# Two edits to the order of work in a transformer kernel's delta-rule phase: a normalisation placed 16 scan instructions earlier on VectorE, and gate products threaded between output products on GpSimd

## The chip, the cores and the metric

One core of one Trainium2 chip runs the whole program. The metric is device time in microseconds (us) of one execution. The kernel before takes 1597.2 us, the median of three runs (1592.9 to 1600.5).

Engines are called PE (TensorE, matmuls and transposes), DVE (VectorE), ACT (ScalarE), POOL (GpSimd) and SP (SyncE, which issues the DMAs). Each executes its own list of instructions in the order in which it was written; they meet only through semaphores.

## The reference

The input is `x` of shape (8, 512, 128). Two layers, each an attention and a feed-forward part, each followed by `layernorm(x + part(x))`:

```
x = ln(x + attention16(x))            # softmax attention, 16 heads of 8
x = ln(x + soft_moe(x))               # 8 experts x 64 slots, gelu
x = ln(x + delta_block(x))            # below
x = ln(x + ternary_mlp(x))            # silu(x W1)*(x W2) -> gelu(. H1) -> gelu(. H2) -> W3
```

`delta_block` holds the only part that is serial in time. For every batch and head a state `S` of 8 x 8 is carried over the 512 time steps:

```
S = S + beta * outer(k, v - S^T k);   o = S^T q
h = x + o @ Wo;   y = rmsnorm(h)
h = h + (silu(y @ Wg) * (y @ Wu)) @ Wd
```

The change touches only the last two lines of the model, which the kernel does together as its second phase.

## The kernel before, in words

Phase one (the first 950 us) does attention and the mixture of experts, batch by batch. The change leaves it as it is.

Phase two handles the 512 time steps in eight blocks of 64. The blocks are worked in a software pipeline of ten steps. While step `t` runs, these blocks are in work:

- **block t: the scan** (DVE, `scan`, lines 1746 to 1782). The 128 batch-head pairs lie on the partitions. The block is cut into 16 chunks of 4 time steps. 12 instructions (L1752 to L1765) prepare all chunks, then every chunk takes 6 dependent ones (L1770, L1772, L1773, L1775, L1777, L1781): 108 in all. Below, n is the count of scan instructions already issued in a step. The state lies in PSUM and ACT copies it away in four quarters (`keep_history`, L1428 and L1429). DVE may overwrite a quarter's state only when it has been copied (semaphore `hist_kept`).
- **block t-1: output and first MLP.** POOL multiplies the kept states with q (`out_products`, L734 and L736; `half` 1 is the second half of the block), DVE sums them (`sum_out`, L1795), SP sends the result through DRAM to transpose it (L577, L581), PE projects it (use `wo`, L1093), DVE adds the residual and makes the factor of the rmsnorm (`residual_h`, L1806 on), POOL applies it (L755), PE transposes (use `hT`), and PE, ACT and POOL do the gated MLP: PE `gates_gu` (L1102), ACT copies (L1378), POOL `gate_gu` (L750), PE `mlp_out` (L1108). PE then does one quarter of another block's layer (`layer_n(last, 3)`, L1116) and transposes the result, use `fo` (`turn_f`, L1085). DVE adds it in `norm_x3` (L1820) and makes the statistics of the layernorm; ACT applies them; PE transposes `x3`.
- **block t-2, called `last`: second MLP.** PE `gates_ab` (L1102), POOL `gate_ab` (L744, one for each quarter `c` of the hidden width), PE `layer_m` for k = 0 to 3, where quarter k waits for `gate_ab` of c = k, then `layer_n`, `last_out`, `turn_y`; DVE `norm_x4` (L1828).

PE's list for a step is: `gates_ab`, `layer_m` 0 to 3, `layer_n` 0 and 1, `project_o` (use `wo`), `layer_n` 2, `turn_h`, `gates_gu`, `mlp_out`, `layer_n` 3, `turn_f`, `last_out`, `turn_y`, `turn_x3`.

On DVE the pieces stand between the scan's instructions at places that are numbers. In its `step`:

```
upto(AT_PAIRS)                 # scan up to n = 12
... sum_out(mlp, 1, r), sum_scores, norms_qk with scan between
upto(AT_H);  residual_h(...)   # n = 31
upto(AT_F);  norm_x3(...)      # n = 83
norm_x4(...)                   # 12 scan instructions threaded through it
upto(AT_S);  sum_out(scanned, 0, r) x4, one scan instruction after each
further(DVE_SCAN)              # the rest
```

`norm_x3` waits for `fo` on PE, and everything behind it on DVE, the scan too, stands still while it waits. `norm_x4` is called with scan instructions between its own dependent ones, `norm_x3` without.

POOL's list for a step is: four `gate_ab` of `last`, four `out_products` of half 1 of block t-1 (the first waits for the fourth quarter of `hist_kept`, so for the end of that block's scan), then `score_products` (L721), `squares2` (L698), `normalise` (L707 to L712), `normalise_h` (L755), four `gate_gu`, and four `out_products` of half 0.

Of the kernel before, what the change touches and what calls it, by code (L numbers as in the profile page):

```python
# [32 lines left out]
HC = HID // P  # L33
QW = 3 * D + NH
CH = 4
# [104 lines left out]
def build(nc, A, out, taps=None):  # L140
    ctx = ExitStack()
    with ctx:
# [477 lines left out]
        def _(g):  # L620
# [73 lines left out]
            def squares2(t, h):  # L694
                g.wait_ge(l_loaded[h], CREDIT + (t - h) * 32 + 64)

                g.wait_ge(norms_done, CREDIT + t * DVE_NORMS)
                g.tensor_tensor(l_sq, mix[:, h, 0:2 * HD, :], mix[:, h, 0:2 * HD, :], ALU.mult).then_inc(l_squared, 1)  # L698

            def normalise(t, h):  # L700


                g.wait_ge(norms_done, CREDIT + (t + 1) * DVE_NORMS)
                r_q, r_k = l_r[:, 0:TS], l_r[:, TS:2 * TS]
                by_time = lambda j: mix[:, h, j * HD:(j + 1) * HD, :].rearrange("p d t -> p t d")
                along = lambda r: r.unsqueeze(2).broadcast_to([P, TS, HD])
                g.tensor_tensor(k_c, by_time(1), along(r_k), ALU.mult).then_inc(l_kb, 1)  # L707
                g.tensor_tensor(wu[h][:, :, 0:HD], by_time(1), along(r_beta), ALU.mult).then_inc(l_kb, 1)
                g.tensor_tensor(wu[h][:, :, HD:2 * HD], by_time(2), along(beta[:, h, :]), ALU.mult).then_inc(l_kb, 1)
                g.tensor_tensor(k_d[:, h, :, :], mix[:, h, HD:2 * HD, :], r_k.unsqueeze(1).broadcast_to([P, HD, TS]),  # L710
                                ALU.mult).then_inc(l_kb, 1)
                g.tensor_tensor(q_c[:, h, :, :], by_time(0), along(r_q), ALU.mult).then_inc(l_kb, 1)  # L712

            def score_products(t, h):

                g.wait_ge(l_kb, CREDIT + (t + 1) * 5)
                g.wait_ge(qkd_done, CREDIT + t)
                qc = q_c[:, h, :, :].rearrange("p (c j) d -> p c j d", j=CH)
                kc = k_c.rearrange("p (c j) d -> p c j d", j=CH)
                for r, at in PAIRS:  # L720
                    last = g.tensor_tensor(qk_m[:, :, at:at + r + 1, :], kc[:, :, 0:r + 1, :],  # L721
                                           qc[:, :, r, :].unsqueeze(2).broadcast_to([P, NC, r + 1, HD]), ALU.mult)
                last.then_inc(qk_made, 1)

            def out_products(t, h, half, r):

                cs = slice(half * HALF, (half + 1) * HALF)
                if r == 0:
                    g.wait_ge(hist_kept, CREDIT + t * 4 + 2 * half + 2)
                    g.wait_ge(om_summed, CREDIT + t * 8)  # L730
                    g.wait_ge(qkd_done, CREDIT + t + 1)
                qc = q_c[:, h, :, :].rearrange("p (c j) d -> p c j d", j=CH)
                _, at = PAIRS[r]
                g.tensor_tensor(o_m[half][r][:, :, :, 0:HD], state[h][:, cs, :, :],  # L734
                                qc[:, cs, r, :].unsqueeze(2).broadcast_to([P, HALF, HD, HD]), ALU.mult)
                g.tensor_tensor(o_m[half][r][:, :, :, HD:HD + r + 1], u_c[h][:, cs, :, 0:r + 1],  # L736
                                qkd[:, h, cs, at:at + r + 1].unsqueeze(2).broadcast_to([P, HALF, HD, r + 1]), ALU.mult) \
                    .then_inc(om_made, 1)

            def gate_ab(t, c):  # L740
                if c == 0:
                    g.wait_ge(a2_ready, CREDIT + t * len(A2.order))
                g.wait_ge(a2_act, CREDIT + A2.emptied(f"b{c}", t))
                g.tensor_tensor(hid_a[:, c, :], up[:, c % 2, :], gate[:, c % 2, :], ALU.mult).then_inc(gated2, 1)  # L744

            def gate_gu(t, c):
                if c == 0:
                    g.wait_ge(a1_ready, CREDIT + t * len(A1.order))
                g.wait_ge(a1_act, CREDIT + A1.emptied(f"u{c}", t))
                g.tensor_tensor(hid_g[:, c, :], up[:, c % 2, :], gate[:, c % 2, :], ALU.mult).then_inc(gated1, 1)  # L750

            def normalise_h(t, h):

                g.wait_ge(h_done, CREDIT + (t + 1) * DVE_H)
                g.tensor_tensor(hn, h1, st_h[:, 5, :].unsqueeze(2).broadcast_to([P, 4, D]), ALU.mult).then_inc(hn_done, 1)  # L755
                g.tensor_tensor(x2t[h], x2t[h], h1, ALU.add).then_inc(x2_added, 1)

            def step(scan, after, mlp, last, h):
                if last is not None:
                    for c in range(HC):  # L760
                        gate_ab(last, c)
                if mlp is not None:
                    for r in range(CH):
                        out_products(mlp, 1 - h, 1, r)
                if scan is not None:
                    score_products(scan, h)
                if after is not None:
                    squares2(after, 1 - h)
                    normalise(after, 1 - h)
                if mlp is not None:  # L770
                    normalise_h(mlp, 1 - h)
                    for c in range(HC):
                        gate_gu(mlp, c)
                if scan is not None:
                    for r in range(CH):
                        out_products(scan, h, 0, r)

            squares2(0, 0)
            normalise(0, 0)
            step(0, 1, None, None, 0)  # L780
            step(1, 2, 0, None, 1)
            with g.Fori(0, 2) as i:
                step(2 * i + 2, 2 * i + 3, 2 * i + 1, 2 * i, 0)
                step(2 * i + 3, 2 * i + 4, 2 * i + 2, 2 * i + 1, 1)
# [1099 lines left out]

QK_TURNED = (1, 3)

AT_PAIRS, AT_H, AT_F, AT_S = 12, 31, 83, 90

W_FIRST = 4 + 4 + 1 + 2 + 1 + 1
W_REST = 2 + 2 + 2 + 4 + 2 + 2 + 2 + 2 + 4  # L1890
# [29 lines left out]
```

## Time and profile before

| | us |
|---|---|
| median of three runs | 1597.2 |
| the profiled execution, device time | 1600.5 |
| its span in the trace | 1598.8 |
| phase two in the trace, first scan instruction to the end | 950.7 to 1598.8 |

The profiled execution is one of the three runs, the slowest. Its steps 1 to 7 of phase two begin at 1004.9, 1072.3, 1143.1, 1217.8, 1289.8, 1361.9 and 1433.2 us; the last scan ends at 1495.8. All times inside the text are microseconds from the start of the span. Where a row is a timeline row, its first number is when the instruction began and the second how long it took; what stands in brackets is how long the engine was idle before it, and what ended that.

### The profile page before, as it was taken

Reading aid. Unit: us, or ns where it says so; the run is one execution under the profiler, and the core shown is the slowest. Engines: PE = TensorE matmul, PEld = TensorE weight load, DVE = VectorE, ACT = ScalarE, POOL = GpSimd, SP = SyncE. Lnnn points to the kernel's source line nnn. Section 1 sums busy time; section 2 is a strip of 40 time slices with the busy share of each in tenths; the row PEclk is TensorE's granted clock in tenths of the full one; section 3 lists DMA queues with packets and bytes.
Section 4 is the critical chain, followed back from the end, with each engine's and each line's share of the span. In section 5 each row is a group of like instructions: output and inputs, shape, how many; then the busy total and the mean of one; then the engine's idle time right before and its main releaser. Section 6 shows DMA issues by size and latency. Waiting matters only on the chain.

```text
span 1598.8 us, 18446 instructions
## 1 busy us (share of the span) xinstructions
PE 1192.1 (75%) x5332; PEld 589.3 (37%) x5332; DVE 990.2 (62%) x2506; ACT 618.3 (39%) x1167; POOL 464.7 (29%) x460
## 2 busy tenths in 40 slices
PE   2288888798888989889796510178977788799987
PEld 1133345363453535445353300033433343333433
DVE  1162835637576374863636239988988899998520
ACT  1115081652817437174363200032534435254452
POOL 0103031210302113030110033555654565555230
PEclk9557597896978969789698755588989889899999
DMA  4302011021201112021000041010101100000000
GB/s 140 105 1 93 8 41 60 1 93 35 85 15 58 62 34 92 7 67 52 28 1 28 28 102 21 13 28 14 28 24 38 35 20 7 20 7 20 20 0 14
DMA packets 81365, 61.72 MB, mean 39 GB/s; under 512 B 40720, under 2 KB 60816, under 8 KB 81296
## 3 DMA queue, kind: packets, MB, share of 16 engines
q1 hardware_dynamic: 81296, 60.92, 13.0%
q8 instruction: 29, 0.48, 0.1%
q14 instruction: 40, 0.33, 0.1%
HBM read 34.69 MB, written 25.95 MB: 38 GB/s over the span
## 4 chain that ended last, share of the span: by engine, by line
PE 44%; DVE 23%; issue 14%; ACT 8%; POOL 8%; DMA 2%; SPq 1%; DVEq 0%; ACTq 0%; POOLq 0%
PE ps L1102 5%; DVE arena L1584 5%; PE ps L813 5%; PE ps L1116 4%; PE ps L875 4%; PE ps L845 3%; ACT arena L1252 3%; PE ps L1108 3%; ACT arena L1214 3%; PE ps L864 2%; PE ps L924 2%; PE ps L848 2%; PE ps L951 2%; PE ps L904 2%; PE ps L942 2%
## 5 line engine op out<-in xcount | busy, mean ns | idle before, releaser
L1214 ACT ACTIVATE arena<-ps 128x512 f32<-128x512 f32 (+2 forms) x200 | 109.9, 573 | 384.2 <-PE ps L813 305.9
L1116 PE MATMUL ps<-arena,f_h 128*128 128x512 f32 x512 | 230.0, 606 | 0.0
L1584 DVE TENSOR_REDUCE arena<-ps 128x2 f32<-128x1024 f32 (+3 forms) x176 | 194.8, 1123 | 36.5 <-PE ps L848 33.3
L668 POOL TENSOR_SCALAR_AFFINE_SELECT arena<-arena 128x512 f32<-128x512 f32 x128 | 84.3, 659 | 386.6 <-ACT arena L1252 386.2
L1252 ACT ACTIVATE arena<-ps 128x1024 f32<-128x1024 f32 (+3 forms) x256 | 170.1, 718 | 38.8 <-PE ps L864 37.3
L845 PE MATMUL ps<-kr,qr 32*128 32x512 f32 (+3 forms) x512 | 123.6, 534 | 48.5 <-DVE arena L1584 24.1
L813 PE MATMUL ps<-ident,arena 128*128 128x128 f32 (+1 forms) x640 | 112.0, 323 | 62.2 <-DVE arena L1525 27.6
L1116 PEld LDWEIGHTS ps<-arena,f_h 128*128 128x128 f32 x512 | 99.6, 196 | 123.3 <-issue 123.3
L1378 ACT ACTIVATE arena<-ps,f_s 128x512 f32<-128x512 f32 x128 | 85.4, 688 | 89.7 <-PE ps L1116 72.3
L1629 DVE RECIPROCAL arena<-ps 128x16 f32<-128x16 f32 x32 | 8.2, 256 | 172.3 <-PE ps L813 172.2
L813 PEld LDWEIGHTS ps<-ident,arena 128*128 128x128 f32 (+1 forms) x640 | 82.2, 159 | 88.3 <-issue 32.5
L875 PE MATMUL ps<-arena 128*32 128x512 f32 (+3 forms) x1024 | 100.0, 476 | 16.5 <-ACT arena L1214 16.5
L1378 ACT ACTIVATE arena<-ps 128x512 f32<-128x512 f32 x96 | 57.0, 597 | 129.7 <-PE ps L1085 56.1
L1093 PE MATMUL ps<-w_o,arena 128*128 128x128 f32 x64 | 13.6, 380 | 120.6 <-DMA arena<-o_d 120.6
L845 PEld LDWEIGHTS ps<-kr,qr 32*128 32x128 f32 x512 | 57.0, 248 | 103.3 <-DVE arena L1584 71.6
L864 PE MATMUL ps<-qr,kr 32*128 32x256 f32 (+3 forms) x512 | 74.2, 435 | 27.9 <-ACT arena L1252 21.5
L734 POOL TENSOR_TENSOR arena<-arena 128x512 f32<-128x512 f32 x64 | 86.2, 1347 | 29.9 <-ACT e_w L1429 29.9
L1616 DVE TENSOR_REDUCE arena<-ps 128x1 f32<-128x512 f32 x64 | 44.1, 689 | 79.9 <-PE ps L904 75.2
L864 PEld LDWEIGHTS ps<-qr,kr 32*128 32x128 f32 x512 | 34.7, 194 | 120.4 <-ACT arena L1252 91.2
L1102 PE MATMUL ps<-arena,f_w 128*128 128x512 f32 x128 | 71.6, 723 | 5.7 <-ACT arena L1378 5.7
L848 PE MATMUL ps<-mask_qk,ident_b 128*128 128x128 bf16 (+2 forms) x352 | 75.7, 313 | 0.0
L744 POOL TENSOR_TENSOR arena<-arena 128x512 f32<-128x512 f32 x32 | 41.1, 1283 | 106.1 <-ACT arena L1378 97.0
(168 smaller groups left out, 2083.6 us busy)
## 6 DMA issues: line engine op xcount, KB each, us to landing
qr<-q_rep SPq DMA_DIRECT2D x8, 1024.0 KB, 5.7
kr<-k_rep SPq DMA_DIRECT2D x8, 1024.0 KB, 7.9
q_rep<-hilo SPq DMA_DIRECT2D x24, 256.0 KB, 3.0
k_rep<-hilo SPq DMA_DIRECT2D x24, 256.0 KB, 3.8
proj_d<-arena SPq DMA_DIRECT2D x8, 768.0 KB, 3.6
arena<-proj_d SPq DMA_DIRECT2D x24, 256.0 KB, 4.1
arena<-in_L_ffn_h_w SPq DMA_DIRECT2D x2, 1024.0 KB, 8.6
arena<-in_L_attn_x SPq DMA_DIRECT2D x8, 256.0 KB, 2.8
```

What stands on the lines that cost most here:

```text
L734: g.tensor_tensor(o_m[half][r][:, :, :, 0:HD], state[h][:, cs, :, :], qc[:, cs, r, :].unsqueeze(2).broadcast_to([P, HALF, HD, HD]), ALU.mult)
L813: last = pe.transpose(bank[0:src.shape[1], k * P:(k + 1) * P], src, ident[:, :])
L845: pe.matmul(bank[:, j, :], qr[rows, gg, it * P:(it + 1) * P], kr[rows, gg, 0:w], start=(j == 0), stop=False)
L848: last = pe.matmul(bank[:, :, it * P:w], ident_b[:, :], mask_qk[:, :].unsqueeze(1).broadcast_to([P, len(gs), P]), start=False, stop=True)
L864: last = pe.matmul(ps[:, 2 * (k % 2) + n, 0:S - jt * P], kr[rows, gg, jt * P:(jt + 1) * P], qr[rows, gg, jt * P:S], start=True, stop=True)
L875: last = pe.matmul(bank[32 * h4:32 * h4 + 32, jt * P:S], v_aug[:, jt, 4 * gg + h4, :], prob[:, gg % 2, h4, p_off[jt]:p_off[jt] + S - jt * ...
L1102: return pe.matmul(ps[:, ring2.bank(use), :], w, src, start=True, stop=True)
L1116: last = pe.matmul(ps[:, ring2.bank(f"{n}{c}"), :], w[:, k, c * P:(c + 1) * P], src[:, k, :], start=(k == 0), stop=(k == HC - 1))
L1214: return act.activation(dst, src(ps[:, bank, :]), func, **kw)
L1252: act.activation(prob[:, gg % 2, 2 * pr:2 * pr + 2, p_off[jt]:p_off[jt] + w], ps[:, bank:bank + 2, 0:w], ACT.Exp).then_inc(p_taken, 1)
L1378: return act.activation(dst, src(ps[:, ring2.bank(use), :]), func, **kw)
L1584: v.tensor_reduce(heads[:, 2 * pr:2 * pr + 2, gs[0]:gs[-1] + 1], ps[:, 2 * (k % 2):2 * (k % 2) + 2, 0:len(gs) * w].rearrange("p q (n w) -> ...
```

## The change

On POOL, the four `gate_ab` of `last` no longer all stand ahead of the `out_products` of half 1. Two stand ahead, the third comes behind the first product pair and the fourth behind the second. On DVE the place of `norm_x3` goes from n = 83 to n = 67.

```diff
@@ gpsimd step @@
-                if last is not None:
-                    for c in range(HC):
+                for c in range(2):
+                    if last is not None:
                         gate_ab(last, c)
-                if mlp is not None:
-                    for r in range(CH):
-                        out_products(mlp, 1 - h, 1, r)
+                for c in range(4):
+                    if mlp is not None:
+                        out_products(mlp, 1 - h, 1, c)
+                    if last is not None and c < 2:
+                        gate_ab(last, c + 2)
@@ constants @@
-AT_PAIRS, AT_H, AT_F, AT_S = 12, 31, 83, 90
+AT_PAIRS, AT_H, AT_F, AT_S = 12, 31, 67, 90
```

POOL, second step of the loop, before (L744 is `gate_ab`, L734 and L736 are one `out_products`, the REGISTER_ALU rows make the number of a semaphore wait):

```order
L743 REGISTER_ALU
L744 TENSOR_TENSOR arena<-arena 128x512
L729 REGISTER_ALU
L734 TENSOR_TENSOR arena<-arena 128x64x8
L736 TENSOR_TENSOR arena<-e_w,arena 128x64
L734 TENSOR_TENSOR arena<-arena 128x64x8
L736 TENSOR_TENSOR arena<-e_w,arena 128x64x2
```

The same place now:

```order
L729 REGISTER_ALU
L734 TENSOR_TENSOR arena<-arena 128x64x8
L736 TENSOR_TENSOR arena<-e_w,arena 128x64
L743 REGISTER_ALU
L744 TENSOR_TENSOR arena<-arena 128x512
L734 TENSOR_TENSOR arena<-arena 128x64x8
L736 TENSOR_TENSOR arena<-e_w,arena 128x64x2
```

The gate product now stands behind the wait (L729) that belongs to the first output product.

DVE, around `norm_x3` in an early step, before (L1773 to L1777 are the third to fifth instruction of a chunk of the scan, L1820 is the first of `norm_x3`):

```order
L1773 TENSOR_TENSOR ps<-arena,ps 128x32
L124 REGISTER_ALU
L1775 TENSOR_TENSOR arena<-ps,arena 128x256
L124 REGISTER_ALU
L1777 TENSOR_REDUCE arena<-arena 128x64
L1729 REGISTER_ALU
L1820 TENSOR_TENSOR arena<-ps,arena 128x512
```

Now, with every line number two higher because the file has two lines more (L1783 is the last instruction of a chunk, L1772 the first of the next, L1822 is `norm_x3`):

```order
L1783 TENSOR_TENSOR ps<-ps,arena 128x64
L124 REGISTER_ALU
L1772 TENSOR_TENSOR arena<-arena,ps 128x256
L1731 REGISTER_ALU
L1822 TENSOR_TENSOR arena<-ps,arena 128x512
L1823 REGISTER_ALU
L1502 BN_STATS arena<-arena 128x6 x4
```

`norm_x3` and, behind it, `norm_x4` moved ahead of 16 scan instructions. Nothing was added or taken away on any engine.

## Rows read from the trace of the kernel before

**Rows 1.** The page: the chain that ended last, shares of the span by engine

```profile
PE 44%; DVE 23%; issue 14%; ACT 8%; POOL 8%; DMA 2%; SPq 1%; DVEq 0%; ACTq 0%; POOLq 0%
```

**Rows 2.** Busy time in step 3: PE, PEld, DVE, ACT, POOL, clock, DMA, GB/s

```profile
1143.00:1218.00 75.00, 63.00 (x144) 27.52 (x143) 66.19 (x181) 30.82 (x59) 42.66 (x39) 0.89 0.10 26
```

**Rows 3.** DVE's waits from 1072 to 1496: total, times, longest

```profile
DVE slot_T L1808 <- ACT arena L1407: 8.1, 6, 1.3
...
DVE arena L1800 <- POOL arena L721: 0.8, 1, 0.8
DVE arena L1820 <- PE ps L1085: 0.6, 1, 0.6
DVE arena L1738 <- POOL arena L698: 0.4, 1, 0.4
```

**Rows 4.** DVE's timeline, step 3: end of residual_h, n=67, n=83, norm_x3

```profile
1174.99 0.16 DVE L1491 SCALAR_TENSOR_TENSOR slot_T<-slot_T 128x4 f32<-128x4 f32 x1
...
1189.07 0.42 DVE L1770 TENSOR_TENSOR arena<-arena,ps 128x256 f32<-128x256 f32 x1
...
1195.38 0.42 DVE L1777 TENSOR_REDUCE arena<-arena 128x64 f32<-128x256 f32 x1
1195.93 0.69 DVE L1820 TENSOR_TENSOR arena<-ps,arena 128x512 f32<-128x512 f32 x1
```

**Rows 5.** PE's timeline, step 3: layer_n 3 and the transposes of fo

```profile
1191.86 3.60 PE L1116 MATMUL ps<-arena,f_h 128*128 128x512 f32 x8
1195.29 0.60 PE L1085 MATMUL ps<-ident,arena 128*128 128x128 f32 x4
```

**Rows 6.** The same pair, PE's fo and DVE's norm_x3, in steps 1, 5, 7

```profile
1050.52 0.66 PE L1085 MATMUL ps<-ident,arena 128*128 128x128 f32 x4 [0.69 <-ACT arena L1378]
1054.76 0.68 DVE L1820 TENSOR_TENSOR arena<-ps,arena 128x512 f32<-128x512 f32 x1
...
1341.53 0.60 PE L1085 MATMUL ps<-ident,arena 128*128 128x128 f32 x4
1342.39 0.68 DVE L1820 TENSOR_TENSOR arena<-ps,arena 128x512 f32<-128x512 f32 x1
...
1476.00 0.60 PE L1085 MATMUL ps<-ident,arena 128*128 128x128 f32 x4
1477.75 0.68 DVE L1820 TENSOR_TENSOR arena<-ps,arena 128x512 f32<-128x512 f32 x1
```

**Rows 7.** POOL's and ACT's timelines around the end of step 3's scan

```profile
1213.07 1.27 POOL L744 TENSOR_TENSOR arena<-arena 128x512 f32<-128x512 f32 x1 [0.44 <-ACT arena L1378]
1214.98 0.27 ACT L1429 ACTIVATE e_w<-ps 128x128 f32<-128x128 f32 x1
1215.50 1.26 POOL L734 TENSOR_TENSOR arena<-arena 128x512 f32<-128x512 f32 x1 [1.16 <-ACT e_w L1429]
...
1223.09 4.13 POOL L721 TENSOR_TENSOR arena<-arena 128x128 f32<-128x128 f32 x4
```

**Rows 8.** PE's timeline, step 4: layers m and n, then project_o

```profile
1212.11 20.76 PE L1116 MATMUL ps<-arena,f_h 128*128 128x512 f32 x48
1239.96 2.07 PE L1093 MATMUL ps<-w_o,arena 128*128 128x128 f32 x8 [7.10 <-DMA arena<-o_d]
```

**Rows 9.** PE in a window: length, busy, granted clock, DMA share, GB/s

```profile
1252.00:1259.00 7.00, 6.24 (x10) 0.52 0.00 0
```

**Rows 10.** PE's and DVE's timelines, step 8: layers, project_o, last sum

```profile
1495.02 20.76 PE L1116 MATMUL ps<-arena,f_h 128*128 128x512 f32 x48
1515.62 1.05 PE L1093 MATMUL ps<-w_o,arena 128*128 128x128 f32 x8
...
1504.15 0.95 DVE L1795 TENSOR_REDUCE arena<-arena 128x64 f32<-128x768 f32 x1 [0.98 <-POOL arena L736]
```

**Rows 11.** DVE's timeline: first three scan instructions of steps 4, 7

```profile
1217.82 2.79 DVE L1752 TENSOR_TENSOR arena<-arena 128x128 f32<-128x128 f32 x3 [3.15 <-issue]
...
1433.18 1.09 DVE L1752 TENSOR_TENSOR arena<-arena 128x128 f32<-128x128 f32 x3
```

## The prediction

> **What bounds the kernel now.** I read the page first, then the busy windows of phase two step by step, then DVE's waits, then the timelines of DVE, PE, POOL and ACT around the two places of the change.
>
> The page's chain gives PE the largest share [rows 1], but that is an average over two phases, and most of PE's part is phase one, which is not touched. In a step of phase two DVE is busy 66.2 of 75 us, PE 63.0 and POOL 42.7 [rows 2]; the rest of DVE's time is mostly the short gap between one scan instruction and the next that needs it. So the question is whether DVE waits for anyone. Between 1072 and 1496 it hardly does [rows 3]: 8.1 us for ACT inside `residual_h` (1.3 each time), and 0.6 us once for PE in front of `norm_x3`. Phase two up to the end of the last scan is bound by DVE's list, and whatever makes DVE stand still there is added to the time, unless a wait further down gives it back.
>
> **The DVE edit: the new wait.** What `norm_x3` waits for is `fo`. In step 3 `residual_h` ends at 1174.99 + 0.16 = 1175.15, and `fo` is ready at 1195.29 + 0.60 = 1195.89 [rows 4, 5]: 20.7 us later, by way of POOL, PE, ACT, POOL and again PE. DVE fills this with scan. It issues n = 83 at 1195.38, ends it at 1195.80, and begins `norm_x3` at 1195.93 [rows 4], with 0.04 us between the end of `fo` and that start. The place is filled to the brim: DVE arrives when `fo` does.
>
> At n = 67 it arrives earlier: the 67th scan instruction ends at 1189.07 + 0.42 = 1189.49 [rows 4], 14.3 us behind the end of `residual_h`, and the 83rd at 1195.80. The 16 between take 6.31 us. Nothing in the edit makes `fo` come sooner: its chain begins at n = 31, whose place is the same. It needs the scan only up to n = 60 (ACT copies the second quarter of the state ahead of its copy for `fo`), and 60 is below 67, so the chain can go on while DVE stands. The new wait is therefore 6.31 us less whatever room there was between the end of `fo` and the start of L1820:
>
> - step 1: `fo` at 1051.18, L1820 at 1054.76 [rows 6], room 3.6: wait 2.7. There is no `last` block in work yet, so PE has no `layer_n` 3 (3.6 us [rows 5]) in front of `fo`.
> - step 2: L1820 already waits 0.6 [rows 3]; it will wait 6.9: 6.3 more.
> - step 3: room 0.04: 6.3.
> - step 5: `fo` at 1342.13, L1820 at 1342.39 [rows 6], room 0.26: 6.05. Steps 4 and 6 are like it; I take 6.1 and 6.2.
> - step 7: `fo` at 1476.60, L1820 at 1477.75 [rows 6], room 1.15: 5.2, treated with the tail.
>
> Steps 1 to 6 give 2.7 + 6.3 + 6.3 + 6.1 + 6.05 + 6.2 = 33.6 us. The amount of work behind the place is the same, since `norm_x4` still threads 12 scan instructions and the four sums one each, so nothing is gained by threading. What is late next is each following step as a whole: DVE's scan ends 6 us later relative to its `residual_h`.
>
> Can it be given back? Only by a wait of DVE that shrinks. All waits of rows 3 are tied to things that DVE itself started shortly before (the 1.3 us for ACT's squares) and shift with it. I count nothing.
>
> **The POOL edit inside the loop.** Before, the fourth gate product begins at 1213.07 and ends at 1214.34; the state's last quarter has been copied at 1215.25, and the first output product starts at 1215.50 [rows 7], 0.8 us behind the scan's end (1214.7). So the gates were through before the wait that now stands in front of two of them. With the scan's end 6.3 us later relative to the gates, the first product starts at about 1221.8 on that clock, the third gate is through 1.6 + 1.2 us later at 1224.6, the fourth 1.8 + 1.2 us later at 1227.6. PE has `layer_m` 0 and 1 done by 1212.11 + 16 x 0.43 = 1219.0 (0.43 us for each of the 48 instructions [rows 8]) and now stands 5.6 us in front of `layer_m` 2. The 32 instructions left then end at 1224.6 + 13.8 = 1238.4. `project_o` waits for its DMA, which follows DVE's sums, and so starts 6.3 us later than before, at 1246.3; it had 7.10 us of idle PE ahead [rows 8] and still has 7.9. The price on the path is 0; the cover is that gap, and if it were used up, each us beyond would delay `residual_h`'s input.
>
> POOL is behind by the two gates, 2.5 us, for the output products 2 to 4 and `score_products`, which began at 1223.09 [rows 7]. DVE has waited for that line and for L698 once, 0.8 and 0.4 us [rows 3], in step 2, where POOL's first output product was 2 us late. Bounds: 0 and 1.2 us in each of six steps, 0 to 7 us; the waits of the steps where POOL was on time are 0, but the margin is under 1 us in the loop, so I take 2 us.
>
> The gates also move beside DVE's 12 preparing instructions, which read SBUF as POOL does. These are unsteady: the first three take 2.79 us in step 4 and 1.09 in step 7 [rows 11]. POOL was already busy without a gap from 1215.50 on, so it is other POOL work that is pushed out behind them. Gain and loss are both possible, 1.7 us a step either way by rows 11, and I take 0. The Trainium skill ("SBUF — State Buffer", section "Who interferes with whom") says that a DVE instruction with two SBUF inputs and a GpSimd instruction exclude each other for the whole instruction. By that rule each of the two gates could hold up one DVE instruction for up to its 1.27 us, 2.5 us a step or 15 us in six; rows 11 agree that such collisions happen, and for the sum they only matter if they are more than before.
>
> **The tail.** Behind the last scan PE is the bound: in step 8 its 48 instructions end and `project_o` starts at 1515.62 [rows 10] although DVE's last sum was done at 1505.1, and the way through DRAM took 5.1 us from such an end (1234.8 to 1239.96 in step 4), so the data were there at about 1510.2. Here the wait of step 7 is partly covered, but the gates are not. With DVE 5.2 us late the scan ends at 1501.0. `layer_m` could start 1.1 us earlier than the 1495.02 of rows 10, and its quarter 2 at 1493.9 + 6.9 = 1500.8; instead gate 2 is through 0.7 + 1.5 + 1.25 us behind the scan's end (products and gates as in rows 7, less the collisions with the scan, which is over), 1504.4. 32 instructions of 0.43 end at 1518.2. The data side: the last product is through at 1501.0 + 0.7 + 6.9 + 2.5 = 1511.1, its sum at 1512.1, its data at 1517.2. `project_o` starts at 1518.2 and not 1515.6: +2.6 us, and all that follows is serial.
>
> **Sum.** 33.6 + 2 + 2.6 = 38 us on the profiled execution's 1600.5, so 1638.7. That execution is 3.3 us above the median of the runs shown, so the median becomes 1597.2 + 38 = 1635. A change of less than 0.5% (8 us) can't be told from none here.
>
> **Rivals.**
> - **PE's clock stays up (faster than my sum, still slower than before).** After idle stretches the granted clock is low: 0.52 in 1252 to 1259 [rows 9], 1.2 GHz, right after 4.6 us of idle PE, just in the chain to `fo`. In step 7 and 8, where it was mostly at 2.4 GHz there, the chain took 19.2 and 18.9 us and not 20.3 to 21.2. If the shifted pauses spared the chain, the waits of steps 2 to 6 would be 1.2 us shorter each: 1635 - 6 = 1629. Against it: the idle time between `project_o` and the transposes of `hn` does not change. The new pause of 5.6 us in front of `layer_m` 2 may lower the clock there; that lengthens work with 7.9 us to spare, and in the tail adds up to 3 us. The Trainium skill ("TensorE: Matmul & The Clock Gate", section "HAM oscillation — how this bites in real kernels") says that a pause between bursts makes the next burst start at the low clock every time; rows 9 agree with it. By that rule the new pause costs in the tail, which stands inside my range.
> - **POOL becomes a second wait.** The backlog of 2.5 us reaches DVE at L1800 or L1738 in every step (7 us and not 2), and collisions cost 1.3 us a step more (8 us): 1635 + 5 + 8 = 1648. For it: step 2, where POOL was late, and rows 11. Against it: from step 3 on POOL was ready each time.
> - **Not slower.** One mechanism: `fo` comes by the time that DVE reaches n = 67, because its chain takes at most 14.3 us. Then the wait is 0 and x3 is in hand 6.3 us earlier, the tail could start 1.1 us sooner, and the time is about 1596. It decides at 14.3 us. Against it: the shortest chain in the trace is 16.7 us (step 1, 1051.18 less 1034.5), without `layer_n` 3, and no instruction of the chain is taken out or moved.
>
> **How the numbers follow.** My forecast (1628 to 1643 by itself, each term within its bounds) 0.68; clock 0.13; POOL 0.14; not slower 0.05, of which faster 0.02 and within 0.5% 0.03. Slower by over 0.5%: 0.95. The range reaches from under the clock case to above the POOL case, 1620 to 1651, and leaves out some 1 in 8.
>
> **What would show it.** In the profile after, DVE's waits should have a row of `norm_x3` (L1822) waiting for PE's L1087, about 7 times and 57 us, of which 19 were there in step 8. The steps 2 to 6 should be 78 us long and not 72. PE should pause about 5 us between the second and the third quarter of `layer_m`, released by POOL's L744. In step 8 `project_o` should start about 17 to 18 us behind the last scan's end. If L1822 waits much less, the chain to `fo` became shorter and I am wrong on the main term; if DVE waits for POOL at L1802 or L1740 the second rival is at work; if `project_o` is late inside the loop, the spare 7.9 us was wrong.

## The result, and the profile after

The changed kernel takes 1638.6 us (median of four runs, 1637.8 to 1641.1) against 1598.4 us before (four runs): ratio 1.026, 95% interval 1.023 to 1.029. It is slower by 40 us; 38 us had been predicted.

The page of the kernel after, for all engines and for the chain that ended last:

```profile
PE 1196.0 (73%) x5332; PEld 588.4 (36%) x5332; DVE 994.8 (61%) x2506; ACT 618.5 (38%) x1167; POOL 463.5 (28%) x460
...
PE 42%; DVE 23%; issue 15%; POOL 8%; ACT 8%; DMA 2%; SPq 1%; DVEq 0%; ACTq 0%; POOLq 0%
```

The chain's shares are those of [rows 1] within two points: nothing in such a page tells where 40 us went. All lines of DVE and most others are numbered two higher than before. The waits of DVE from the first step to behind the last scan do tell it (line, who was waited for, total, times, longest):

```profile
DVE arena L1822 <- PE ps L1087: 36.9, 7, 6.8
DVE slot_T L1810 <- ACT arena L1409: 9.4, 7, 1.3
...
DVE arena L1830 <- PE ps L1087: 3.0, 6, 0.5
DVE arena L1802 <- POOL arena L721: 2.0, 1, 2.0
```

`norm_x3` (L1822) waits in each of the seven steps, 36.9 us in all; before it was 0.6 us in one step [rows 3]. DVE's timeline in step 3 shows one of these waits, between the 67th scan instruction and `norm_x3`:

```profile
1201.83 0.42 DVE L1772 TENSOR_TENSOR arena<-arena,ps 128x256 f32<-128x256 f32 x1
1208.80 0.69 DVE L1822 TENSOR_TENSOR arena<-ps,arena 128x512 f32<-128x512 f32 x1 [6.55 <-PE ps L1087]
```

and PE's timeline what it waits for, the last quarter of layer n and then the transposes of `fo`:

```profile
1204.73 3.60 PE L1118 MATMUL ps<-arena,f_h 128*128 128x512 f32 x8
1208.16 0.60 PE L1087 MATMUL ps<-ident,arena 128*128 128x128 f32 x4
```

`fo` is ready at 1208.76, 20.8 us behind the end of `residual_h` (1187.9), where it was 20.7 us in [rows 4, 5]. The chain to `fo` is as long as it was; DVE comes to it earlier and stands.

The other edit shows in POOL's timeline at the end of the same scan (1233.9). The two later gates (L744) now stand behind a product pair each:

```profile
1234.75 1.26 POOL L734 TENSOR_TENSOR arena<-arena 128x512 f32<-128x512 f32 x1 [11.05 <-ACT e_w L1431]
1235.97 0.33 POOL L736 TENSOR_TENSOR arena<-e_w,arena 128x64 f32<-128x64 f32 x1
1236.26 1.26 POOL L744 TENSOR_TENSOR arena<-arena 128x512 f32<-128x512 f32 x1
...
1239.41 1.58 POOL L744 TENSOR_TENSOR arena<-arena 128x512 f32<-128x512 f32 x1
```

and in PE's, which pauses for the first of them and still has time to spare in front of `project_o` (L1095); before, 48 instructions ran without a pause [rows 8]:

```profile
1224.90 7.03 PE L1118 MATMUL ps<-arena,f_h 128*128 128x512 f32 x16
1237.58 7.75 PE L1118 MATMUL ps<-arena,f_h 128*128 128x512 f32 x14 [5.65 <-POOL arena L744]
...
1258.68 2.07 PE L1095 MATMUL ps<-w_o,arena 128*128 128x128 f32 x8 [5.63 <-DMA arena<-o_d]
```

Phase one, which is the same code in all these kernels, ends anywhere between 945 and 954 us from one profile to the next. So profiles are compared below by phase two alone, from the first scan instruction to the end of the span: 648.1 us before (950.7 to 1598.8), 686.4 after (953.0 to 1639.4), 38.3 us more.

### The profile page after: what moved, and what is told of

The parts are those of the page before. It is cut to its first block, busy times and chain, and to the rows that moved or that the text cites. A ratio compares the mean times of both kernels' runs of the same rounds, so it can differ in the third digit from the quotient of the medians.

```text
span 1639.4 us, 18446 instructions
## 1 busy us (share of the span) xinstructions
PE 1196.0 (73%) x5332; PEld 588.4 (36%) x5332; DVE 994.8 (61%) x2506; ACT 618.5 (38%) x1167; POOL 463.5 (28%) x460
## 4 chain that ended last, share of the span: by engine, by line
PE 42%; DVE 23%; issue 15%; POOL 8%; ACT 8%; DMA 2%; SPq 1%; DVEq 0%; ACTq 0%; POOLq 0%
PE ps L1104 5%; DVE arena L1586 5%; PE ps L815 4%; PE ps L1118 4%; PE ps L877 4%; PE ps L847 3%; PE ps L1110 3%; ACT arena L1216 3%; ACT arena L1254 3%; PE ps L866 2%; PE ps L926 2%; PE ps L906 2%; PE ps L850 2%; PE ps L953 2%; PE ps L944 2%
## 5 line engine op out<-in xcount | busy, mean ns | idle before, releaser
L1118 PE MATMUL ps<-arena,f_h 128*128 128x512 f32 x512 | 242.3, 630 | 40.6 <-POOL arena L744 40.6
L1118 PEld LDWEIGHTS ps<-arena,f_h 128*128 128x128 f32 x512 | 102.9, 204 | 172.8 <-issue 125.3
L734 POOL TENSOR_TENSOR arena<-arena 128x512 f32<-128x512 f32 x64 | 85.9, 1342 | 98.5 <-ACT e_w L1431 98.5
L1095 PE MATMUL ps<-w_o,arena 128*128 128x128 f32 x64 | 11.0, 325 | 112.5 <-DMA arena<-o_d 112.5
L1087 PE MATMUL ps<-ident,arena 128*128 128x128 f32 x128 | 23.8, 316 | 67.3 <-POOL arena L755 44.0
L1104 PE MATMUL ps<-arena,f_w 128*128 128x512 f32 x128 | 67.8, 690 | 5.7 <-ACT arena L1380 5.7
```

Source lines behind the costliest of these rows:

```text
L1104: return pe.matmul(ps[:, ring2.bank(use), :], w, src, start=True, stop=True)
L1118: last = pe.matmul(ps[:, ring2.bank(f"{n}{c}"), :], w[:, k, c * P:(c + 1) * P], src[:, k, :], start=(k == 0), stop=(k == HC - 1))
```

## The experiments

The question for the first four is: is the loss DVE's wait, what does POOL's order do, and what sets the length of the wait.

**1. Only the DVE edit.** From the kernel before:

```diff
-AT_PAIRS, AT_H, AT_F, AT_S = 12, 31, 83, 90
+AT_PAIRS, AT_H, AT_F, AT_S = 12, 31, 67, 90
```

> The kernel before with norm_x3 at n = 67 and POOL's order as it was. Theory (DVE waits at norm_x3 for a fo that comes no sooner): waits of 2.7, 6.3, 6.3, 6.1, 6.05, 6.2 us in steps 1 to 6 and 5.2 in step 7, the last hidden in the tail where PE is the bound, which gains 1 us; 33.6 - 1 = 33 us more than before, about 1631 us. Rival (a good part of the 40 us comes from the POOL order, because PE then stands 36 us in all for gate products): under 1620 us.

Measured: 1637.1 us, ratio 1.0246 (1.0227 to 1.0265); phase two 684.9 us, 36.8 more than before. The rival is out: this edit alone is nearly the whole loss. It is 6 us more than expected. DVE's waits in this run:

```profile
DVE arena L1820 <- PE ps L1085: 37.5, 7, 6.0
```

33.4 of the 37.5 us lie in steps 1 to 6, against 33.6 expected plus the 0.6 that was there, so the main term was right. What was missed is in the 12 preparing scan instructions: in step 2 they took 8.8 us before and 11.8 here (see experiment 8). In step 1 the chain to `fo` took 18.2 us and not 16.7, at a mean granted clock of PE of 0.75 and not 0.82, which cost 1.5. The two make 4.4 of the 6 us. About 2 us more fell in step 5, where two instructions of `norm_x4` on 128 x 4 elements took 1.25 and 1.14 us beside gate products on POOL, instead of 0.15 each.

**2. Only the POOL edit.** From the changed kernel, with the place of `norm_x3` set back:

```diff
-AT_PAIRS, AT_H, AT_F, AT_S = 12, 31, 67, 90
+AT_PAIRS, AT_H, AT_F, AT_S = 12, 31, 83, 90
```

> The kernel before with only POOL's gate products threaded between output products, norm_x3 at n = 83. Theory: the gates still come before layer_m needs them or cost only spare PE time, the sums in the tail come 2.5 us later with 5 us to spare: 1598 us, no change within 2 us. Rival (POOL order carries a good part of the loss by itself): 1605 to 1620 us, with PE pauses in front of layer_m of over 3 us a step.

Measured: 1596.1 us, ratio 0.9994 (0.9981 to 1.0006): no change, as the theory had it. In this run PE has no wait for a gate product in any row of the waits from 1072 to 1500. By itself the reordering costs nothing that the times show, since the gates are there before PE wants them. POOL's delay does reach DVE: it waits twice 2.0 us for the score products (L721), where it waited 0.8 us once before.

**3. norm_x3 at n = 75**, half way, POOL as before:

```diff
-AT_PAIRS, AT_H, AT_F, AT_S = 12, 31, 83, 90
+AT_PAIRS, AT_H, AT_F, AT_S = 12, 31, 75, 90
```

> The kernel before with norm_x3 at n = 75, half way. Theory: the place is 3.15 us of scan earlier, less the room: 0 in step 1, 3.15, 3.1, 2.9, 2.9, 3.0 in steps 2 to 6, tail -1: 14 us more than before, about 1612 us. Rival (the cost is that of DVE's order as such, not of time standing in front of fo): not in proportion, near 1598 or near the 1631 of n = 67.

Measured: 1619.4 us, ratio 1.0124 (1.0103 to 1.0146). DVE's wait:

```profile
DVE arena L1820 <- PE ps L1085: 18.6, 7, 3.5
```

0.6, 18.6, 37.5 us at n = 83, 75, 67: the wait grows in proportion to the scan taken away in front of it, and the time with it (0, 20, 39 us by the ratios). The expected 14 us were too few by the first two things of experiment 1: step 1 waits 1.5 us, and the 12 preparing instructions of step 2 take 11.8.

**4. Both edits, and the last quarter of layer n behind fo on PE:**

```diff
                 if mlp is not None:
                     mlp_out(mlp, turn)
-                if last is not None:
-                    layer_n(last, turn, 3)
                 if mlp is not None:
                     turn_f(mlp, turn)
                 if last is not None:
+                    layer_n(last, turn, 3)
                     last_out(last, turn)
```

> The changed kernel (both edits) with PE's last quarter of layer n put behind the transposes of fo instead of ahead. Theory (the wait is as long as the chain from residual_h to fo, and these 3.6 us of PE stand in it, of which 2.5 are not hidden by ACT's copy): fo 2.5 us sooner in steps 2 to 8, waits of about 3.7 us and not 6.2, 12.5 us less in the loop and 2.5 to 5 less in the tail: about 1622 us. Rival (the chain is held by something else, POOL or the end of the scan): 1636 to 1640 us.

Measured: 1645.0 us, ratio 1.0291 (1.0273 to 1.0309), so 6 us slower than the change and not 17 us faster. The expected effect on `fo` is there, in step 3 it comes 18.3 us behind `residual_h` and not 20.8. DVE's waits (its lines are one higher than before in this kernel):

```profile
DVE arena L1821 <- PE ps L1087: 25.2, 7, 4.4
DVE arena L1829 <- PE ps L1087: 12.5, 6, 2.2
```

The first wait fell by 11.7 us, and the second, of `norm_x4` for `y`, rose by 9.5 (3.0 after the change). `y` needs the moved quarter as well; in step 3 it now comes 0.9 us later, since PE pauses 0.69 us for ACT's copy in front of `fo`. And `norm_x3`, started sooner, now runs beside POOL's output products: from its start to the end of the scan it is 28.6 us in steps 2 to 5, and 25.1 in the changed kernel. DVE's timeline in step 3:

```profile
1209.15 0.39 DVE L1505 TENSOR_TENSOR slot_T<-arena 128x4 f32<-128x4 f32 x1
1209.47 1.31 DVE L1506 TENSOR_TENSOR slot_T<-arena 128x4 f32<-128x4 f32 x1
1210.71 0.72 DVE L1507 TENSOR_TENSOR slot_T<-arena 128x4 f32<-128x4 f32 x1
```

Three instructions that take 0.16 us each in the kernel before take 2.4 us together. My theory of a single wait fell: DVE has two things to wait for there, and shortening the way to the first hands most of the wait on. The rival fell too, since the time rose above its 1640 us.

**5. The same on the kernel before** (n = 83), to see the second part alone:

> The kernel before with PE's last quarter of layer n behind the transposes of fo, norm_x3 at n = 83. In the run with both edits this made fo 2.4 us sooner and the time 6 us longer. Theory A (fo is only the first of two things that DVE waits for here; y, for norm_x4, comes 0.8 us later since PE now pauses for ACT's copy of fT): DVE waits 0.8 us a step more for y, about 1603 us. Theory B (fo alone counts): no change in the loop and 2.5 us gained in the tail, 1595 us.

Measured: 1603.7 us, ratio 1.0038 (1.0023 to 1.0052), the time of theory A. `fo` came up to 4.7 us before DVE wanted it. DVE's wait for `y` in the kernel before and in this one:

```profile
DVE arena L1828 <- PE ps L1085: 2.0, 5, 0.5
...
DVE arena L1827 <- PE ps L1085: 4.6, 5, 1.8
```

So fewer than the 0.8 us a step of theory A: 1.3 us more in step 2, 0.8 in step 3, 0.3 or less from step 4 on, 2.6 us in all. Phase two is 3.9 us longer (652.0 against 648.1). Up to the start of step 7 it is 1.6 us; the rest came behind it, where the 12 preparing instructions took 12.4 us and not 9.4. Theory B is out, but the time agrees with theory A partly by luck.

**6. Use the time instead: scan instructions threaded through norm_x3**, at n = 83. The call is given the same threading that `norm_x4` has:

```diff
-                    norm_x3(mlp, 1 - h, order(ln3_done, DVE_LN, mlp, False))
+                    norm_x3(mlp, 1 - h, order(ln3_done, DVE_LN, mlp, True))
```

> The kernel before with 12 scan instructions threaded through norm_x3, at n = 83. Theory (DVE's list bounds the loop and norm_x3's small dependent instructions waste their gaps): norm_x3 to norm_x4 takes 4.8 us and 12 scan instructions 4.7 us; threaded together 6.4 us as norm_x4 does; 3.1 us less in each of 7 steps, 2 us more in the tail and up to 1 us a step for POOL coming later: 1580 to 1586 us. Rival (the circle of PE, ACT and POOL from residual_h back to residual_h takes over): 1593 us or more, with DVE waiting for project_o.

Measured: 1613.8 us, ratio 1.0114 (1.0086 to 1.0141). The theory fell, and so did the rival's account of it. DVE waits 0.3 us in all for `fo` and not at all for `project_o` in the loop. It waits here:

```profile
DVE ps L1781 <- ACT e_w L1429: 37.0, 7, 6.0
```

L1781 is the last instruction of the scan. It overwrites the third quarter of the state, which ACT must have copied. ACT's timeline at the end of step 3's scan (1216.2) shows where that copy (L1428, L1429) stood:

```profile
1203.48 1.65 ACT L1412 ACTIVATE arena<-arena,slot_T 128x128 f32<-128x128 f32 x4 [2.41 <-DVE slot_T L1815]
...
1214.82 0.69 ACT L1378 ACTIVATE arena<-ps,f_s 128x512 f32<-128x512 f32 x1 [0.17 <-PE ps L1102]
1215.41 0.38 ACT L1428 ACTIVATE arena<-ps 128x256 f32<-128x256 f32 x1
1215.67 0.28 ACT L1429 ACTIVATE e_w<-ps 128x128 f32<-128x128 f32 x1
```

It is behind the six ACT copies for `gate_ab` (L1378), which follow from `norm_x3` itself. In the kernel before that copy ended 2.7 us ahead of L1781 (1211.7 against 1214.4 in step 3). Threaded, DVE can reach L1781 5.2 us sooner behind the start of `norm_x3` (13.5 us and not 18.7 to the end of the scan; experiment 9 shows it without the wait), and the copy ends 3.1 us later behind that start, 2.1 of them since ACT gets the statistics later. 5.2 + 3.1 - 2.7 is the 5.6 us that DVE waits in step 3. The wait belongs to neither edit of the change.

**7. residual_h threaded as well**, `norm_x3` at n = 91:

```diff
-                    residual_h(mlp, 1 - h, order(h_done, DVE_H, mlp, False))
+                    residual_h(mlp, 1 - h, order(h_done, DVE_H, mlp, True))
```

> As the run with the threaded norm_x3, and residual_h threaded too, norm_x3 at n = 91, so that it still meets fo. Theory (DVE bounds): another 3 us a step, 1565 us. Rival (the circle fo 20.5, norm_x3 6.4, applying, transposing and copying 3.2, gates 8.8, layers 20.8, project_o 1.5, residual_h 6.8 us makes 68 us and the step can't be shorter): 5 us less than the run before it at most, with DVE waiting at project_o or POOL.

Measured: 1648.7 us, ratio 1.0319 (1.0287 to 1.0351). The same copy is waited for, 54.6 us in the first six of the steps. Both theories left it out.

**8. What POOL's work does to DVE's preparing instructions.** POOL's output products of half 1 are held back until DVE has issued the 12:

```diff
+                    if scan is not None:
+                        g.wait_ge(scan_done, CREDIT + scan * DVE_SCAN + 12)
                     for r in range(CH):
                         out_products(mlp, 1 - h, 1, r)
```

> The kernel before with POOL's output products of half 1 held back until DVE has issued the 12 preparing instructions of the next scan. It measures the collision of the two: theory (POOL's products beside them cost 3 us a step): the 12 take 9 us or less in every step and not 11.8; DVE then waits for POOL's late products, 1610 to 1625 us in all. Rival (the 11.8 us are DVE's own): 11.8 stays.

Measured: 1617.8 us (one run). The 12 take 7.4 or 7.5 us in six of the steps 1 to 7 and 8.3 in the other. Before it was 11.8 us in steps 3, 5 and 6. The theory held, for the time too: DVE now waits 36 us for the late products (L1797, L1802). The first instructions of step 3, in this run:

```profile
1152.85 1.10 DVE L1754 TENSOR_TENSOR arena<-arena 128x128 f32<-128x128 f32 x3 [0.23 <-DVE ps L1783]
...
1155.89 0.69 DVE L1764 TENSOR_TENSOR arena<-arena 128x512 f32<-128x512 f32 x1
```

and in the kernel before:

```profile
1143.10 2.17 DVE L1752 TENSOR_TENSOR arena<-arena 128x128 f32<-128x128 f32 x3 [0.23 <-DVE ps L1781]
...
1147.65 1.64 DVE L1762 TENSOR_TENSOR arena<-arena 128x512 f32<-128x512 f32 x1
```

So the collision costs up to 4.4 us a step (11.8 less 7.4) and is in the time of the kernel before already. How much it costs depends on how the two lists lie against each other. In step 2 of the kernel before POOL was 2 us further back in its list, and the 12 took only 8.8 us, though POOL was busy from 0.7 us behind their start; with `norm_x3` earlier POOL starts its products on time there too, and the 12 take as long as in the next steps (11.8 and 11.5 us). This is a cost of the DVE edit that was not in my sum. Why the first position costs DVE less is not shown.

**9. Threaded norm_x3 and ACT's copy first.** Experiment 6, and on ACT:

```diff
+                if mlp is not None:
+                    keep_history(mlp, 1 - h, 2)
                 if last is not None:
                     for c in range(3):
                         take_ab(last, c)
-                if mlp is not None:
-                    keep_history(mlp, 1 - h, 2)
```

> As the run with the threaded norm_x3 at n = 83, and ACT copies the third quarter of the state ahead of its six copies for gate_ab and not behind them. Theory (the 37 us that DVE waited at the last scan instruction were ACT's list: the copy stood behind work that follows norm_x3): that wait goes, the 3.1 us a step of threading stay, 1578 to 1586 us. Rival (the circle over PE, ACT and POOL is the bound at 70 us or more a step): 1594 us or more, DVE waiting elsewhere.

Measured: 1589.4 us, ratio 0.9936 (0.9922 to 0.9950), faster than before, and between the theory's range and the rival's. The wait of 37 us is gone. Steps 1 to 6 are 14.7 us shorter than before, of the 18.6 that threading should give there. Behind the start of step 7 it takes 170.4 us instead of 165.6. DVE's waits from 1005 to 1530 are now

```profile
DVE arena L1800 <- POOL arena L721: 11.7, 6, 2.2
...
DVE arena L1795 <- POOL arena L736: 10.5, 9, 6.7
```

Of the second row only 1.0 us lies ahead of the last scan's end; 9.5 us are behind it. Inside the loop it is the score products (L721) that DVE waits for.

**10. The same with the change's POOL order:**

> As the run before it with POOL's gate products threaded between output products, as in the change. Theory (now the scan ends before the gates are through, so output products that stand behind two gates instead of four start up to 2.5 us earlier): 0 to 5 us less than the run without. Rival (POOL's order is worth nothing here either): the same within 2 us.

Measured: 1599.4 us, ratio 1.0006 (0.9994 to 1.0018), so the POOL order costs about 10 us here, and both the theory and the rival fell. Phase two is 648.4 us against 638.3, all of it in steps 1 to 6. DVE's wait for the products went from 10.5 to 27.7 us (from 1.0 to 16.6 ahead of the last scan's end). The first product still waits for the last quarter of the state, which ACT copies behind all its work for the gates; so it does not start sooner (7.5 us behind the end of step 3's scan, and 8.1 here), and the two gates in between make the other three later. My expectation had overlooked that ACT's order ties the two.

**11. residual_h threaded too, n = 91, ACT's copy first** (the edits of experiments 7 and 9 together):

> residual_h threaded as well, norm_x3 at n = 91, ACT's copy first. Theory (circle of about 68 us a step): no more than 5 us below the run with norm_x3 alone threaded, DVE waiting for project_o, for POOL's sums or for the copy. Rival (DVE alone bounds): 15 us or more below it.

Measured: 1603.7 us (one run); phase two 648.2 us, 10 more than in experiment 9. The theory of the circle is right only in that nothing was gained, and the rival (DVE alone bounds) fell. Towards the end of the scan `norm_x4` and the sums have no scan instructions left to be threaded with: from the end of a scan to the next one it takes 4.6 to 5.8 us inside the loop, where experiment 9 has 2.2 to 3.6 and the kernel before 0.2 to 3.1. Also `residual_h` itself takes 7.9 us and not 6.8, which makes everything behind it later.

**12. Experiment 9, and score_products moved to where POOL was idle:**

```diff
-                if scan is not None:
-                    score_products(scan, h)
...
                 if mlp is not None:
                     normalise_h(mlp, 1 - h)
+                if after is not None:
+                    score_products(after, 1 - h)
```

(and one call for block 0 ahead of the first step).

> As the run with the threaded norm_x3 and ACT's copy first (1589.4 us), and POOL's score_products of the next block moved from behind the output products to the gap between normalise_h and gate_gu, where POOL was idle about 5 us. Theory (two things cost there: DVE waits 2.0 us a step at L1800 for the score products, and they collide with DVE's 12 preparing instructions): L1800's wait goes, 2 to 3 us a step in six steps, 1571 to 1580 us. Rival (the circle over PE, ACT and POOL already bounds the step, so DVE's waits only change their place): 1586 us or more.

Measured: 1578.9 us, ratio 0.9872 (0.9852 to 0.9893), the fastest of all; phase two 625.5 us. From 1072 to 1490 DVE waits, in this kernel's lines:

```profile
DVE arena L1797 <- POOL arena L736: 10.6, 9, 6.8
DVE arena L1808 <- PE ps L1095: 8.5, 5, 3.4
```

The theory held: the wait for the score products is gone. All but 1.1 us of the first row lie behind the last scan's end (1470.6). The 8.5 us for `project_o` are new: here the circle from `residual_h` over PE, ACT and POOL back to it begins to bind in five of six steps.

## Why the prediction was right, point by point

- **DVE's list bounds the loop.** Right: experiments 1 and 3 make DVE stand still there and the time follows. The prediction named two waits of DVE and passed over a third, 2.0 us for `y` (L1828, the row in experiment 5). It went to 3.0 us, which is small, but experiment 4 shows that it takes over as soon as `fo` comes sooner.
- **The wait at norm_x3.** Right in mechanism and nearly in size. Step by step, predicted and measured: 2.7 and 2.7; 6.9 and 6.1; 6.3 and 6.6; 6.1 and 4.6; 6.05 and 6.0; 6.2 and 6.8; step 7 5.2 and 4.1. Steps 1 to 6 waited 32.8 us in all. In step 4 the chain to `fo` took 18.9 us and not 20.3. That is the rival of PE's clock in one step: the granted clock was 0.66 (that is, partly 1.2 and partly 2.4 GHz) from 1270 to 1275, where the chain begins, and 1.00 from then on. In the other steps up to 6 the wait was within 0.8 us of my forecast.
- **"I count nothing" given back.** Right inside the loop; the 8.1 us for ACT in six steps of [rows 3] are there unchanged.
- **The POOL edit inside the loop.** The pause of PE came as worked out (5.65 us in step 4, 5.6 predicted). The spare time left in front of `project_o` was 5.6 us and not 7.9: 1.6 of the 2.3 us are the lower clock behind the pause, where the 32 instructions took 15.5 us and not 13.8. The 2 us for POOL's backlog did not come in steps 1 to 6. DVE waited there 1.2 us for POOL before (in step 2) and not at all after; its one wait of 2.0 us at L1802 is in step 7. Steps 1 to 6 together are 35.0 us longer than before with both edits and 37.4 us with the DVE edit alone. One profile each stands behind that difference of 2.4 us, and it agrees with a chain to `fo` that was 1.5 us shorter in step 1 and 1.1 in step 4, so a gain by the POOL order is not shown.
- **The tail.** The scan ends at 1539.3 and the gate for quarter 2 is through so that PE resumes 3.5 us later, as worked out (1504.4 less 1501.0). PE's timeline:

```profile
1531.72 7.03 PE L1118 MATMUL ps<-arena,f_h 128*128 128x512 f32 x16
1542.81 16.45 PE L1118 MATMUL ps<-arena,f_h 128*128 128x512 f32 x32 [4.06 <-POOL arena L744]
1559.09 1.05 PE L1095 MATMUL ps<-w_o,arena 128*128 128x128 f32 x8
```

  But the 32 instructions took 16.3 us, not 13.8. PE in windows behind the pause (length, busy, granted clock, DMA share, GB/s):

```profile
1539.00:1543.00 4.00, 0.19 (x1) 0.74 0.00 0
1543.00:1550.00 7.00, 7.00 (x11) 0.66 0.00 0
1550.00:1559.00 9.00, 9.00 (x22) 1.00 0.36 87
```

  The rule of the Trainium skill that I had weighed, that a burst behind a pause starts at the low clock ("TensorE: Matmul & The Clock Gate", section "HAM oscillation — how this bites in real kernels"), is borne out here, with 2.5 us. So `project_o` started 19.8 us behind the scan's end, as it did before, and not 17 to 18 as the prediction had given for a sign. PE's row in the run with the DVE edit alone, without a pause:

```profile
1529.24 20.76 PE L1116 MATMUL ps<-arena,f_h 128*128 128x512 f32 x48
1551.64 1.16 PE L1093 MATMUL ps<-w_o,arena 128*128 128x128 f32 x8 [1.64 <-DMA arena<-o_d]
```

  Here `project_o` starts 13.6 us behind the scan's end (1538.1). With the scan's end itself, 0.7 us later in its step, the POOL order makes `project_o` 7.0 us later once `norm_x3` is early. 3.1 us of it came back at the very end, which is luck: the 16 gate instructions of the last block, in the kernel before and in the changed one,

```profile
1547.37 9.57 PE L1102 MATMUL ps<-arena,f_w 128*128 128x512 f32 x16 [0.69 <-ACT arena L1378]
...
1590.38 7.13 PE L1104 MATMUL ps<-arena,f_w 128*128 128x512 f32 x16 [0.69 <-ACT arena L1380]
```

  take 10.2 us in the run with the DVE edit alone. PE sat idle for 0.7, 1.4 and 0.7 us ahead of them in all three, yet the granted clock was 0.81 before (1539 to 1557), 0.80 with the DVE edit alone (1576 to 1593) and 1.00 in the changed kernel (1583 to 1597). From the start of step 7 to the end it is 168.9 us with both edits, 165.1 with the DVE edit alone and 165.6 before.
- **The sum.** 35.6 us for steps 1 to 6 were predicted and 35.0 measured, 2.6 and 3.3 for the rest. The main term, the wait, is shown. That the small terms add up is luck in both places. In steps 1 to 6 the waits were 1.4 us less than forecast and POOL's 2 us did not come; in their place the 12 preparing instructions took 2.7 us more in step 2 and 0.3 to 0.6 us less in each of steps 3 to 6, and in step 6 two instructions on 128 x 4 elements took 1.20 and 1.13 us beside a gate product instead of 0.15. I had put all collisions at 0. In the tail, predicted and measured: the scan's end 5.2 and 6.2 us later (4.1 at `norm_x3`, 2.0 at L1802); from there to `project_o` 2.6 us less and no change; from `project_o` to the end no change and 2.9 us less (83.2 and 80.3 us), by the clock.
- **The signs.** The prediction's 57 us for L1822 in about 7 waits is a slip, its own terms give 58 in 8; measured were 55.9 in 8, 19.0 of them in step 8. Steps 2 to 6 are 76.3 to 81.0 us long, 78.4 on average, as predicted.
- **What the POOL order is worth on top of the early norm_x3** is not told apart from nothing by the times: 1638.6 us with both edits and 1637.1 with the DVE edit alone, with overlapping intervals.
- **The rivals.** Not slower: out, the shortest chain to `fo` in the loop was 16.7 us in step 1 and 18.0 us else. POOL as a second wait: out, 2.0 us in all. PE's clock: seen in step 4 alone, 1.5 us and not 6.

## What to carry to other kernels

Work that waits for another engine's chain costs nothing while something useful stands ahead of it in the list, and costs the full time of whatever is taken from there: compare the two arrival times in the trace. Here they agreed within 0.3 us in five of the seven steps, and each earlier place lost what was taken away (experiments 1 and 3). A faster engine then meets the next thing that others owe it, which the profile before hardly shows as a wait (here a copy far down in ACT's list: 1.0 us once before, then 37 us); look for every semaphore behind the place and ask who signals it and what stands ahead of that. Reordering that is free where its inputs are early stops being so once another edit moves them: the same POOL order cost nothing on the kernel before, made `project_o` of the last block 7.0 us later with an early `norm_x3` (though the whole time only 1.5 us longer, which is within the noise), and cost 10 us with the threaded one. And a total that comes out right does not vouch for its terms: add up the stages one by one.

## What the runs showed of the hardware

DVE instructions with two operands in SBUF are slowed by POOL's products beside them: the 12 preparing instructions of a scan took 7.4 us without them and 11.8 us with them, and instructions on 128 x 4 elements up to 1.31 us instead of 0.16. Those with one operand in PSUM are not, though POOL runs beside about half of them. All 96 of the first instruction of a chunk in the kernel before (duration in ns, least, median, most):

```profile
L1770 DVE TENSOR_TENSOR arena<-arena,ps x96: 403/420/422, 1081.2 to 1493.5; 128x256 f32<-128x256 f32 x96
```

Two operands are not the whole condition. In `residual_h` of the kernel before, two TENSOR_SCALAR instructions, which read one small tensor each, are slow too. In steps 3 and 7:

```profile
1170.39 1.07 DVE L1808 TENSOR_SCALAR slot_T<-slot_T 128x4 f32<-128x4 f32 x1 [1.35 <-ACT arena L1407]
1171.49 1.19 DVE L1484 TENSOR_SCALAR slot_T<-slot_T 128x4 int32<-128x4 int32 x1
...
1455.70 0.17 DVE L1808 TENSOR_SCALAR slot_T<-slot_T 128x4 f32<-128x4 f32 x1 [1.34 <-ACT arena L1407]
1455.90 0.17 DVE L1484 TENSOR_SCALAR slot_T<-slot_T 128x4 int32<-128x4 int32 x1
```

In steps 1 to 6 POOL runs `normalise` (L707 to L712) beside them, in step 7 it is idle. With the instruction behind them (L1485, 1.26 us and 0.16) this makes `residual_h` 6.8 us long and not 3.8: 3 us in each of six steps, on the list that bounds the loop. No run moved that POOL work away, so what this would gain is not shown.
